# A mixture-of-experts decoder layer: the ring of result rows from four buffers to eight

## What is computed

```python
logits = (flat @ gate_W.T).astype(jnp.float32)
probs = jax.nn.softmax(logits, axis=-1)
top_v, top_i = jax.lax.top_k(probs, K)                      # K = 2 of E = 8 experts
gates = jnp.zeros((T, e), probs.dtype).at[jnp.arange(T)[:, None], top_i].set(top_v)
g = jax.nn.silu(jnp.einsum('td,edf->etf', flat, w1_e))      # D = 128, F = 512
u = jnp.einsum('td,edf->etf', flat, w3_e)
out_e = jnp.einsum('etf,efd->etd', g * u, w2_e)
routed = jnp.einsum('te,etd->td', gates, out_e).reshape(b, s, d)
...
return alpha * shared + (1.0 - alpha) * routed              # shared: 8 small experts for all tokens
x = _layernorm(x + _L0_ffn_ref(...))
```

## Time and profile before

| | |
|---|---|
| median of 3 timed runs | 742.11 us (740.82 to 743.23) |
| span of the profiled execution | 804.8 us |
| TensorE busy in it | 695.4 us, 86% |
| GpSimd busy in it | 481.7 us, 60% |
| first to last e_y copy (71 blocks) | 328.24 to 726.90 us |
| scatters / gathers of the experts' stage | 142 / 108 |

### The profile page before, as it was taken

How to read it: one execution, slowest core, us unless ns; L and a number is a source line. 1 busy time by engine, 2 the same in 40 slices (tenths; PEclk the granted TensorE clock), 3 DMA queues, 4 the chain that set the end, 5 groups by cost and what they waited for, 6 DMA issues and landing times.

```text
span 804.8 us, 16374 instructions
## 1 busy us (share of the span) xinstructions
PE 695.4 (86%) x5111; PEld 641.2 (80%) x5112; DVE 509.8 (63%) x1426; ACT 475.5 (59%) x1434; POOL 481.7 (60%) x471
## 2 busy tenths in 40 slices
PE   5899999979799988989898997998897898899900
PEld 3688888867688877989888996898897897798800
DVE  2689999769999724554454652554544563455995
ACT  4999999823798522544444552454444553445785
POOL 3398888962111476467667886677676687442332
PEclk8999999889999999999999997999999999799965
DMA  8468555533011162111111111111111112116493
GB/s 218 119 195 253 181 178 163 183 108 115 27 53 54 52 162 69 28 44 43 44 44 43 43 42 46 40 47 44 40 47 43 38 44 46 30 57 158 136 263 85
DMA packets 87268, 73.00 MB, mean 91 GB/s; under 512 B 10066, under 2 KB 72410, under 8 KB 87194
## 3 DMA queue, kind: packets, MB, share of 16 engines
q1 hardware_dynamic: 77808, 53.43, 22.5%
q0 software_dynamic: 9088, 18.63, 8.5%
q10 hardware_dynamic: 298, 0.01, 0.0%
HBM read 50.14 MB, written 21.89 MB: 90 GB/s over the span
## 4 chain that ended last, share of the span: by engine, by line
PE 69%; DVE 11%; issue 9%; ACT 6%; DMA 2%; POOL 1%; another core or an unknown queue 0%; SPq 0%; ACTq 0%; POOLq 0%; DVEq 0%
PE bank L1506 16%; PE bank L1471 9%; PE bank L1470 9%; PE bank L1472 9%; PE bank L547 5%; PE bank L1142 3%; PE bank L542 3%; PE bank L1131 2%; ACT ev L708 2%; PE bank L1462 2%; DVE xg L1800 2%; PE bank L1132 2%; PE bank L1133 2%; PE bank L572 2%; PE bank L567 1%
## 5 line engine op out<-in xcount | busy, mean ns | idle before, releaser
L1591 DVE TENSOR_TENSOR s_hT<-s_sg,bank 128x512 f32<-128x512 f32 x142 | 97.3, 687 | 199.9 <-PE bank L1472 87.9
L1422 POOL DMA_INDIRECT y_rows<-e_y,dst_tab x142 | 163.2, 1150 | 86.8 <-ACT e_y L1538 49.6
L1414 POOL DMA_INDIRECT xg<-x_rows,src_tab x142 | 147.7, 1040 | 61.5 <-issue 39.5
L1470 PE MATMUL bank<-e_x_hi,e_w_hi 128*128 128x256 f32 x568 | 175.2, 309 | 9.7 <-issue 9.4
L1471 PE MATMUL bank<-e_x_lo,e_w_hi 128*128 128x256 f32 x568 | 164.2, 289 | 11.2 <-issue 11.0
L1472 PE MATMUL bank<-e_x_hi,e_w_lo 128*128 128x256 f32 x568 | 164.3, 289 | 6.7 <-issue 6.7
L1506 PE MATMUL bank<-w,s_hT 128*128 x1136 | 145.8, 281 | 5.9 <-issue 5.9
L1506 PEld LDWEIGHTS bank<-w,s_hT 128*128 128x128 f32 x1136 | 138.5, 197 | 8.3 <-issue 8.0
L1532 ACT ACTIVATE s_sg<-bank 128x512 f32<-128x512 f32 x142 | 84.8, 597 | 89.3 <-PE bank L1472 42.6
L1471 PEld LDWEIGHTS bank<-e_x_lo,e_w_hi 128*128 128x128 f32 x568 | 111.7, 197 | 15.2 <-issue 15.2
L1472 PEld LDWEIGHTS bank<-e_x_hi,e_w_lo 128*128 128x128 f32 x568 | 111.4, 196 | 9.6 <-issue 9.6
(11 more groups left out here) (168 smaller groups left out, 1463.8 us busy)
## 6 DMA issues: line engine op xcount, KB each, us to landing
yk<-y_rows SPq DMA_DIRECT2D x16, 512.0 KB, 4.5
xT_in<-in_xT_dram SPq DMA_DIRECT2D x16, 256.0 KB, 3.3
x_res<-in_x_dram SPq DMA_DIRECT2D x16, 256.0 KB, 3.4
w_all<-in_L_ffn_w_e_dram SPq DMA_DIRECT2D x16, 256.0 KB, 4.0
c_in<-in_ctx_dram SPq DMA_DIRECT2D x16, 256.0 KB, 2.9
cT_in<-in_ctxT_dram SPq DMA_DIRECT2D x16, 256.0 KB, 3.1
x_rows<-x SPq DMA_DIRECT2D x16, 256.0 KB, 2.4
x2T_cols<-x2T SPq DMA_DIRECT2D x16, 256.0 KB, 2.9
```

What stands on the lines that cost most here:

```text
L1414: nc.gpsimd.indirect_dma_start(xg[b % XR][:, t, :], None, x2_rows, bass.IndirectOffsetOnAxis(src_tab[:, i:i + 1], 0)).then_inc(gathered[b ...
L1422: nc.gpsimd.indirect_dma_start(y_rows, bass.IndirectOffsetOnAxis(dst_tab[:, n:n + 1], 0), y[b % R][:, t, :], None).then_inc(scattered[b % ...
L1470: nc.tensor.matmul(at, w_hi[b % WR][:, w], x_hi[r][:, :], start=True, stop=False)
L1591: nc.vector.tensor_tensor(hT[par][:, half * HC:(half + 1) * HC, :].rearrange("p c n -> p (c n)"), sg[half][:, :], bank[2 + half][:, :], AL ...
```

## The change

The result rows get a ring of their own length, YR = 8, in place of RING = 4. `y` has eight buffers, there are eight semaphores of landed scatters, and `take_y(b)` waits for the scatters of block b - 8. At the end SyncE waits for eight semaphores in place of four. The PSUM bank of the result still alternates with the block's parity. The rings of the rows (x_hi, x_lo, RING = 4), of the weights (3) and of the gathered rows (16) stay. The instructions of all engines stay in their order; only what e_y's copies wait for is another.

```diff
-            scattered = [sem(f"e_scattered{n}") for n in range(RING)]
+            scattered = [sem(f"e_scattered{n}") for n in range(YR)]
...
-XR, RING = 16, 4
+XR, RING, YR = 16, 4, 8
...
-    y = ring("y", [P, BT, D])
+    y = ring("y", [P, BT, D], n=YR)
...
             nc.gpsimd.indirect_dma_start(y_rows, bass.IndirectOffsetOnAxis(dst_tab[:, n:n + 1], 0),
-                                         y[b % R][:, t, :], None).then_inc(scattered[b % R], 16)
+                                         y[b % YR][:, t, :], None).then_inc(scattered[b % YR], 16)
...
-        def take_y(b, j, r):
+        def take_y(b):
             act.wait_ge(y_ps, b + 1)
-            if b >= R:
-                act.wait_ge(scattered[r], 16 * BT * j)
-            nc.scalar.activation(y[r][:, :, :].rearrange("p t d -> p (t d)"), bank[4 + r % 2][:, 0:BT * D],
+            if b >= YR:
+                act.wait_ge(scattered[b % YR], 16 * BT * (b // YR))
+            nc.scalar.activation(y[b % YR][:, :, :].rearrange("p t d -> p (t d)"), bank[4 + b % 2][:, 0:BT * D],
                                  ACT.Copy).then_inc(y_ok, 1)
...
-                take_y(b - 2, j + (r - 2) // R, (r - 2) % R)
+                take_y(b - 2)
...
-        for n in range(RING):
-            sp.wait_ge(scattered[n], 16 * BT * len(range(n, NB, RING)))
+        for n in range(YR):
+            sp.wait_ge(scattered[n], 16 * BT * len(range(n, NB, YR)))
```

## The result

The ring of eight takes 764.63 us (762.87 to 765.72), the kernel before 741.89 us (740.82 to 743.23): a ratio of 1.029, interval 1.026 to 1.032. The prediction said 742.0, with a range of 738 to 745.5. It is wrong by 22.6 us and on the other side of its range; what happened is its rival 2, at more than three times the price written there.

What follows compares the result with a forecast made beforehand. The prediction took TensorE to bound the kernel, with 69% of the chain. Its terms summed to 804.8 + 0 us for the profiled span; it named 742.0 us for the timed runs, range 738 to 745.5.

Steps and rivals of the forecast that it cites:

- rival 2: At L1414 and L1422, a TensorE running ahead makes GpSimd's instructions slower: about +6 us, 748 us; chance 0.10.
- 7.5 us margin: Block 27's copy: the scatter it needs landed 7.5 us before it, the smallest margin found.
- term (1) of the sum: Ring of four to eight in the copy's wait: removes 0 us, bounds 0 and 19.5 us.
- 744.6: Profiled span of 804.8 less 60.2 us of TensorE breaks between blocks; within 0.4% of the 742.11 median.
- leave no visible room for time lost to a full ring: Timed runs look as if TensorE ran its blocks nearly without a break, at 4.88 us each.
- some 3.5 us late: Estimated slack of ScalarE's copy before TensorE notices at the start of the next block.
- 34.2: GpSimd's lag behind the copy, in us, at which a ring of eight is full; 14.7 for four.
- tension: GpSimd's 5.92 us a block would leave unbroken TensorE 64 us ahead: cheaper GpSimd instructions, or the ring fills.
- 0 to 1.6 us: What a deeper ring would gain at the stage's end if the ring of four did fill.
- no ring shortens its list: GpSimd's 250 scatters in fixed order, counted at 1.285 us a step, set the end if the ring fills.
- with a full ring the pattern may be just as bad: Argument against GpSimd's 2.0 us instructions costing more with the deeper ring.
- parts 2 to 4: ScalarE's four fewer waits, SyncE's eight waits, four more tiles and semaphores: 0 us, the last within -0.5 and +0.5.

Runs made afterwards that it cites:

- e8_before: The kernel before, unchanged, profiled on a chip of the kind where it takes 742 us: 744.17 us.
- e7_ring8_no_wlow: Changed kernel's ring of eight, VectorE's L1580 replaced by a 128x16 subtraction from block 3 on (wrong results): 739.4 against 742.15 us for the kernel before.

## Why the prediction was wrong

**The wait that never held.** "In the profiled execution, then, no copy waits for a scatter" was right of that execution, and its 7.5 us margin too. It was carried to the timed runs, where, by e8_before, 48 copies do; term (1) of the sum, put at 0, measured 22.7 us the other way. I had the sign of it in hand: 62.7 us between the span and the median. I put them down to the profiler, without a row that said so. The later profiles have spans of 762.2 and 742.2 us, and their executions took 763.9 and 744.0: the profiler costs nothing to speak of, and the kind of chip does.

**TensorE's step.** 4.88 us a block unbroken was right, to the second digit. The 744.6 us worked out from it meets e8_before's 743.96, but partly by luck. The two spans, 804.8 and 742.2 us, are 62.6 apart: 56.1 of it lies between the first and the last copy (398.7 against 342.6 us) and 6.8 ahead of the first (328.24 against 321.41). The prediction put 60.2 into the first and nothing into the second. And the inference "leave no visible room for time lost to a full ring" failed: the ring can be full at little cost to TensorE. The copy may be some 3.5 us late before TensorE notices (my own estimate). In e8_before ScalarE stands up to 4.0 us for a landing, block after block, and TensorE is busy 345.3 of the 347.6 us from 321.4 to 669.0 all the same; its stage is 4.5 us longer than the 338.1 of e7_ring8_no_wlow.

**The lag.** 5.92 us a block and 1.04 us lost in each were right: in the changed kernel GpSimd's lag rises to 35.8 us (block 34: copy at 487.37, first scatter at 523.18) and the ring of eight fills at block 38, where 34.2 / 1.04 gives 33 and the estimate with the 3.5 us of slack 36. My "tension" between this lag and the 744.6 was the real question. I named two answers: that GpSimd's instructions are cheaper, or that the ring fills, for 0 to 1.6 us. The ring does fill, but the price was wrong, and the two are not apart: it is the full ring that makes GpSimd's instructions cheaper. That stood in rival 2 alone.

**The step that failed: "no ring shortens its list".** The 250 instructions and their order are fixed, but not their durations: 290.0 us in one kernel and 270.2 in the other. I had counted them all at 1.285 with the pause, and the hold of 1.03 us in one of three only under rival 2. So "0 to 1.6 us" faster, for the case that the ring fills, came out as 19.8 us of GpSimd's time slower.

**Rival 2** had the mechanism, its place (L1414 and L1422), the point from which it decides and the 19 blocks. It was mis-sized by its second factor. I took 0.58 us a block, the unbroken stretch's 1.04 less the mean of the profile; but that mean came from a trace in which TensorE's breaks interrupt the pattern. With a full ring the surplus is small (from 405 to 505 us e8_before's 76 instructions take 77.15 us, 1.02 each), so each of the 20 blocks cost nearly the whole 1.0: 19.8 us. Halving it for the case that GpSimd is not the bound was wrong as well: it was. I gave it 0.10 because "with a full ring the pattern may be just as bad". The timeline of a copy that follows a landing could have been worked through, and was not.

**The rule on the ports.** The Trainium skill ("SBUF — State Buffer", Who interferes with whom) says that a VectorE instruction with two SBUF inputs and a GpSimd instruction that reads SBUF exclude each other for the length of an instruction. That it would make this change slower was written beside rival 2. The runs agree where VectorE's instruction began first: 1168 to 975 ns a scatter without L1580, and a hold that shrinks with the instruction's length. Where GpSimd's began first they show no exclusion: L1580 begins under it and neither is longer (46 times in e8_before, above). And under VectorE's L1591, one of whose two inputs lies in PSUM, 83 gathers and scatters begin in e8_before, and none takes over 1.00 us. The same page infers that such a VectorE instruction does not hold up the making of descriptors; for these indirect transfers, whose table lies in SBUF, it does, 2.02 against 0.97 us.

**TensorE and the gathers.** Not foreseen at all: from 553 us on, the changed kernel's TensorE waits for gathered rows, since these stand in GpSimd's queue behind the scatters.

```profile
PE bank L1462 <- DMA xg<-x_rows,src_tab: 13.2, 8, 2.6
```

That view has no such row in e8_before. It is a symptom, not a second cost: GpSimd is not idle in that time, the end is set by its list in either case, and the 19.8 us account for the span's 20.0.

**What the change removed and added beside that** (parts 2 to 4) was worth 0 as forecast, as far as can be measured: 743.06 against 742.15 with the eight buffers, the semaphores and SyncE's eight waits.

## What to carry to other kernels

A buffer ring that is full is not always a loss: the wait can be what sets two engines' instructions in step. Before it is lengthened, see which engine fell behind and why; if an instruction of it is held by another engine's, splitting that one (128x1024 into two of 128x512) cut the longest hold from 1.06 to 0.46 us here, and then the longer ring cost nothing against the kernel before. And a profile whose span is not the timed median must be explained before anything is read from it; a margin in it says nothing of the runs that are timed.

## What the runs showed of the hardware

- Chips differ by 8% on the same program: 742 us on some, 799 to 804 on others, where TensorE has breaks of up to 1.7 us with nothing to wait for that the profile shows, in the experts' stage above all. On those no ring or split made a difference of over 0.6%. Why is open.
- A GpSimd gather or scatter of 128 rows takes 0.97 us; one that begins up to 1.0 us after a VectorE subtraction of 1.23 us from two SBUF operands began takes until about 0.85 us after that one ends (442.41 + 2.04 - 442.36 - 1.23 = 0.86). One that began before it is not held, nor is the subtraction (433.77 for 0.97 us, 433.93 for 1.22).
- Two engines with loops of their own can lock: one held GpSimd instruction and two others, with the pauses, are 4.86 us, to the 4.88 us of a block. In the changed kernel 35 of the first 38 blocks go by with such a long instruction.
